# A two-layer sequence model on one core: a product moved to GpSimd, sums, row maxima and a projection in other places, and the end in another order

## The reference, cut to what matters

```python
xn = layernorm(x)
# layer 0: a selective scan with 16 states over 256 channels, beside a top-1 mixture of 8 experts
hs, gate = split(xn @ in_proj_w.T, 2)                       # 256 wide each
u  = silu(conv1d_depthwise(hs, conv_w, taps 4) + conv_b)
x_dbl = u @ x_proj_w.T                                      # 64 + 16 + 16
dt = softplus(rmsnorm(x_dbl[:64]) * dt_ln_w @ dt_proj_w.T + dt_proj_b)
Bm, Cm = rmsnorm(x_dbl[64:80]) * b_ln_w, rmsnorm(x_dbl[80:]) * c_ln_w
h_t[n] = exp(-dt * exp(A_log[n])) * h_{t-1}[n] + dt * u * Bm[n]       # along the sequence
y = sum_n h[n] * Cm[n] + u * D
x = x + (y * silu(gate)) @ out_proj_w.T + expert_e(xn)      # e = argmax of the gate's logits
xn = layernorm(x)
# layer 1: attention in a window of 32 to both sides, 16 heads of 8, beside a SwiGLU block of 384
q, k, v = xn @ Wq + bq, xn @ Wk + bk, xn @ Wv + bv
p = softmax(q k^T / sqrt(8) + mask(|i - j| <= 32))
x = x + (p v) @ Wo + bo + (silu(xn @ wg.T) * (xn @ wu.T)) @ wd.T
```

## Time and profile before

| | |
|---|---|
| median of three runs | 1000.43 us (1000.12, 1000.43, 1002.18) |
| the profiled execution's own time | 1001.08 us |
| its span in the profile | 999.3 us |
| TensorE busy (matmuls) | 797.0 us, 80% of the span |
| TensorE weight loads | 548.1 us, 55% |
| VectorE busy | 758.9 us, 76% |
| ScalarE busy | 638.5 us, 64% |
| GpSimd busy | 437.8 us, 44% |
| mean granted clock of TensorE | 0.928 of full speed |
| chain that ended last, by engine | PE 36%, DVE 20%, POOL 15%, issue 13%, ACT 9%, DMA 3% |

### The profile page before, as it was taken

The page is one execution under the profiler, slowest core; times in us unless marked ns, Lnnn a source line. Parts: engine busy times, 40 slices in busy tenths (PEclk is TensorE's granted clock), DMA queues, the critical chain, the costliest instruction groups (busy, mean ns, idle before and its releaser), DMA issues.

```text
span 999.3 us, 15614 instructions
## 1 busy us (share of the span) xinstructions
PE 797.0 (80%) x5226; PEld 548.1 (55%) x5226; DVE 758.9 (76%) x1059; ACT 638.5 (64%) x1976; POOL 437.8 (44%) x248
## 2 busy tenths in 40 slices
PE   0955689677489798979898989898988996798775
PEld 0732678676165366546555655565556554555543
DVE  7569445543577988899888888998898788887485
ACT  0224356644269767966796689578947893795563
POOL 2257432110556337624851584258425852672100
...
GB/s 209 189 119 189 206 265 310 244 213 153 65 123 97 85 100 134 104 80 121 130 93 97 127 124 70 106 129 131 52 124 142 104 47 121 157 112 23 18 11 12
DMA packets 85952, 123.20 MB, mean 123 GB/s; under 512 B 8560, under 2 KB 43760, under 8 KB 85744
## 3 DMA queue, kind: packets, MB, share of 16 engines
...
...
## 4 chain that ended last, share of the span: by engine, by line
PE 36%; DVE 20%; POOL 15%; issue 13%; ACT 9%; DMA 3%; SPq 3%; DVEq 0%; POOLq 0%; ACTq 0%
POOL hc L1221 8%; DVE hst L823 7%; PE y_bank L1319 4%; PE more L1451 4%; PE work L1338 4%; DVE dBu L815 3%; POOL xs_d L1189 3%; ACT pexp L1123 3%; POOL x_res L1205 2%; SPq L604 2%; ACT dA L1045 2%; PE work L1364 1%; PE work L1297 1%; PE work_l L1290 1%; PE work L1463 1%
## 5 line engine op out<-in xcount | busy, mean ns | idle before, releaser
L1221 POOL TENSOR_TENSOR hc<-hst,bcr 128x1024 f32<-128x1024 f32 x116 | 276.9, 2387 | 397.6 <-DVE dBu L815 375.3
L823 DVE TENSOR_TENSOR_SCAN hst<-dA,dBu 128x1024 f32<-128x1024 f32 x128 | 291.7, 2279 | 0.9 <-ACT dA L1045 0.3
L1045 ACT ACTIVATE dA<-dt,neg_a 128x511 f32<-128x511 f32 x256 | 170.7, 724 | 13.3 <-DVE hst L823 10.7
L815 DVE TENSOR_TENSOR dBu<-dtu,bcr 128x1024 f32<-128x1024 f32 x128 | 161.8, 1264 | 19.6 <-DMA bcr<-bc_d 9.7
L1319 PE MATMUL y_bank<-pk,hc 128*128 128x128 f32 x1024 | 144.2, 287 | 27.1 <-POOL hc L1221 26.3
L1319 PEld LDWEIGHTS y_bank<-pk,hc 128*128 128x128 f32 x1024 | 122.2, 148 | 64.8 <-POOL hc L1221 39.4
L1451 PE MATMUL more<-pk,pexp 128*96 128x128 f32 x480 | 103.5, 290 | 26.2 <-ACT pexp L1123 20.7
L1451 PEld LDWEIGHTS more<-pk,pexp 128*96 128x96 f32 x480 | 56.5, 125 | 66.1 <-issue 29.2
L1136 ACT COPY pT<-more 96x512 f32<-96x512 f32 x120 | 69.9, 583 | 34.5 <-PE more L1451 34.2
L1123 ACT ACTIVATE pexp<-work_l,nmax 128x96 f32<-128x96 f32 x240 | 78.5, 345 | 9.5 <-DVE nmax L970 9.4
L1123 ACT ACTIVATE pexp<-work,nmax 128x96 f32<-128x96 f32 x240 | 77.7, 335 | 2.6 <-DVE nmax L970 2.6
...
## 6 DMA issues: line engine op xcount, KB each, us to landing
bcr<-bc_d SPq DMA_DIRECT2D x128, 512.0 KB, 5.1
...
```

Source lines behind the costliest of these rows:

```text
L815: v.tensor_tensor(dBu[:], dtu[par], bcr[n % RING][:, 0:1, :].to_broadcast([P, NH, L]), ALU.mult).then_inc(s_dBu, 1)
L823: v.tensor_tensor_scan(hst[n % 2][:].rearrange("p h t -> p (h t)"), dA[n % 2][:].rearrange("p h t -> p (h t)"), dBu[:].rearrange("p h t -> ...
L1045: s.activation(dA[n % 2][:, h, 1:L], dt[par][:, h, 1:L], ACT.Exp, scale=neg_a[:, h, n:n + 1]).then_inc(s_dA, 1)
L1221: g_.tensor_tensor(hc[n % 2][:], hst[n % 2][:], bcr[n % RING][:, 1:2, :].to_broadcast([P, NH, L]), ALU.mult).then_inc(s_hc, 1)
```

## The change

It does the following.

1. The product with C of state 15 goes from VectorE's `step` to GpSimd's `times_c`, which then waits for scan 15.
2. `up2` of sequences 0 to 5 goes from bank 0 to bank 5, the pre lane's bank. `xnT` of the pre lane now waits until `up2` has been read.
3. In slots 7, 8 and 10 the sum stands behind the transposes `turn`. The row maximum of slot 8 stands directly behind the scan.
4. `xdr` goes from the end of slot 9 to directly behind scan 8 in slot 10, and `bc` to the end of slot 10. That holds for turn -1 too.
5. The SwiGLU chunks of sequence 6 leave turn 7 and go to the head of `LAST`, with banks of their own (`FFN_BANK`). `rdT` of that sequence stands behind them.
6. In `LAST` the SwiGLU chunks of sequence 7 go to t = 2 to 7, with buffers of their own (`fth_of`, `fsg_of`, `fh_of`), `avg` to 7, the four `fin` blocks to 8 to 11 one by one, `ffn_down` in four units to 12 to 15. The finish is written out, with the values of groups 13, 14 and 15 in three banks.

```diff
-MID = {2: [("scan", "slots", 0)], 8: [("pre", "ss", 0)], 18: [("pre", "dw", 0)], 20: [("pre", "dt", 0)], 23: [("pre", "dtu", 0)]}
+MID = {2: [("scan", "slots", 0)], 8: [("pre", "ss", 0)], 10: [("pre", "xdr", 0)], 18: [("pre", "dw", 0)], 20: [("pre", "dt", 0)], 23: [("pre", "dtu", 0)]}
...
-        9: [("pre", "xdr", 0), ("pre", "bc", 0), ("scan", "rows", 1)],
-        10: [("pre", "zg0", 0)], 11: [("pre", "sg0", 0), ("scan", "rows", 2)],
+        9: [("scan", "rows", 1)],
+        10: [("pre", "bc", 0), ("pre", "zg0", 0)], 11: [("pre", "sg0", 0), ("scan", "rows", 2)],
...
-ROWMAX_MID = (20,)
+ROWMAX_MID = (8, 20)
+SUM_LAST = (7, 8, 10)
...
+LAST_AT = {0: [("v2", 0), ("v3", 0)],
+           2: [("fg", 0), ("fu", 0)], 3: [("fs", 0), ("fh", 0)], 4: [("fg", 1), ("fu", 1)], 5: [("fs", 1), ("fh", 1)],
+           6: [("fg", 2), ("fu", 2)], 7: [("fs", 2), ("fh", 2), ("avg", 0)],
+           8: [("fin", 0)], 9: [("fin", 1)], 10: [("fin", 2)], 11: [("fin", 3), ("y_out", 0)],
+           12: [("ffn_down", 0)], 13: [("ffn_down", 1), ("proj", 0)], 14: [("ffn_down", 2), ("proj", 1)], 15: [("ffn_down", 3)]}
...
-        units += [("scan", "sum", m) for m in range(N - 1) if SUM_AT[m] == slot]
+        sums = [("scan", "sum", m) for m in range(N - 1) if SUM_AT[m] == slot]
+        units += sums if slot not in SUM_LAST else []
...
         units += [(lane, "turn", g) for lane, g in of("exp", slot)]
+        units += sums if slot in SUM_LAST else []
...
-    out = [("y_end", 0, a), ("rdT", 0, f), ("gated", 0, a), ("yT", 0, a)]
-    out += [(name, 0, a) for name in ("out", "x1", "ln_a", "ln_b", "q", "k", "v0", "v1")]
+    out = [("y_end", 0, a), ("fg", 0, f), ("fu", 0, f), ("gated", 0, a), ("fs", 0, f), ("fh", 0, f), ("yT", 0, a),
+           ("fg", 1, f), ("out", 0, a), ("fu", 1, f), ("x1", 0, a), ("ln_a", 0, a), ("fs", 1, f), ("fh", 1, f),
+           ("fg", 2, f), ("fu", 2, f), ("ln_b", 0, a), ("fs", 2, f), ("fh", 2, f), ("rden", 0, f), ("rdT", 0, f)]
+    out += [(name, 0, a) for name in ("q", "k", "v0", "v1")]
...
+    out += [(name, k, a) for name, k in (
+        ("exp", G - 1), ("scale", G - 2), ("turn", G - 2), ("values", G - 3), ("proj", 2), ("own", G - 4),
+        ("scale", G - 1), ("turn", G - 1), ("own", G - 3), ("values", G - 2), ("y_last", 2), ("own", G - 2),
+        ("values", G - 1), ("own", G - 1), ("proj", 3), ("y_last", 3))]
...
-           "oL": 0, "gate0": 1, "up0": 2, "gate1": 0, "up1": 1, "gate2": 2, "up2": 0}
+           "oL": 0, "gate0": 1, "up0": 2, "gate1": 0, "up1": 1, "gate2": 2, "up2": 5}
...
+FFN_BANK = {"gate0": 5, "up0": 6, "gate1": 7, "up1": 5, "gate2": 6, "up2": 7}
...
             if key == "xnT":
-                done1(eng, b + LAG["pre"] - 1 - LAG["finish"], "fin")
+                done1(eng, b + LAG["pre"] - 1 - LAG["attn"], f"up{HC - 1}")
...
+                    if it == B - 1 and lane == "attn" and name in FFN_UNITS:
+                        continue
...
-                if n == N - 1:
-                    dve.wait_ge(s_h, b * N + N)
-                    dve.wait_ge(s_hc, b * N + N - 1)
-                    dve.wait_ge(s_ys, b * (N + 1) + N - 1)
-                    v.tensor_tensor(hc[n % 2][:], hst[n % 2][:], bcr[n % RING][:, 1:2, :].to_broadcast([P, NH, L]),
-                                    ALU.mult).then_inc(s_hc, 1)
...
-                pool.wait_ge(s_dBu, b * N + n + 2)
+                if n < N - 1:
+                    pool.wait_ge(s_dBu, b * N + n + 2)
+                else:
+                    pool.wait_ge(s_h, b * N + N)
...
-                    if name == "product" and k < N - 1 and not ((b == 0 and k < DVE_C)):
+                    if name == "product" and not ((b == 0 and k < DVE_C)):
                         times_c(b, k)
```

More of the change, by code:

```diff
@@ L215, in keys @@
     return {"scores": [f"s{k}"], "turn": [f"pT{k}"], "fg": [f"gate{k}"], "fu": [f"up{k}"], "ln_b": ["xnT"], "fin": ["fin"] if k == NT - 1 else [], "yT": ["yT0", "yT1"],
-            "values": ["oL" if k == G - 1 else "oK"], "proj": [f"fin{k}"] if k >= 2 else []}.get(name, [])
+            "values": [{G - 3: "oK", G - 2: "oM", G - 1: "oL"}.get(k)], "proj": [f"fin{k}"] if k >= 2 else []}.get(name, [])
 L1_BANK = {"yT0": 1, "yT1": 2, "out": 0, "xnT": 1, "q": 0, "k": 1, "v0": 2, "v1": 0, "v2": 1, "v3": 2, "rdT": 2, "fin": 5,
            **{f"s{k}": k % 2 for k in range(G)}, **{f"pT{k}": 2 for k in range(G)},
-           "oL": 0, "gate0": 1, "up0": 2, "gate1": 0, "up1": 1, "gate2": 2, "up2": 0}
+           "oL": 0, "gate0": 1, "up0": 2, "gate1": 0, "up1": 1, "gate2": 2, "up2": 5}
 LAST_BANK = {"yT0": 1, "yT1": 2, "out": 0, "xnT": 1, "q": 3, "k": 4, "v0": 2, "v1": 6, "v2": 7, "v3": 5,
              **{f"s{k}": (0, 1, 3, 4)[k % 4] for k in range(G)}, **{f"pT{k}": (2, 6)[k % 2] for k in range(G)},
-             "oK": 0, "oL": 1, **{f"gate{k}": 5 for k in range(HC)}, **{f"up{k}": 7 for k in range(HC)}, "fin2": 5, "fin3": 7}
+             "oK": 0, "oM": 3, "oL": 1, **{f"gate{k}": 5 for k in range(HC)}, **{f"up{k}": 7 for k in range(HC)}, "fin2": 5, "fin3": 7}
+FFN_BANK = {"gate0": 5, "up0": 6, "gate1": 7, "up1": 5, "gate2": 6, "up2": 7}
 L1_ORDER = [(turn - LAG[lane], key) for turn in range(1, B) for lane, name, k in PLAN
-            if lane in ("attn", "late", "finish") and 0 <= turn - LAG[lane] for key in keys(name, k)]
+            if lane in ("attn", "late", "finish") and 0 <= turn - LAG[lane]
+            and not (turn == B - 1 and lane == "attn" and name in FFN_UNITS) for key in keys(name, k)]
 L1_ORDER += [(b, key) for name, k, b in LAST for key in keys(name, k)]
@@ L234, in l1_bank @@
         return LAST_BANK[key]
+    if b == B - 2 and key in FFN_BANK:
+        return FFN_BANK[key]
     return L1_BANK[key]
@@ L390, in program @@
         o_last = hst[0][:, 0, :]
+        fh_last = [dA[0][:, 0, :], dA[0][:, 1, :], dA[1][:, 0, :]]
         k_flat_b = rbuf[:, 1, :]
@@ L980, in layer1 @@
                         done1(dve, b, f"up{k - 1}")
-                    v.scalar_tensor_tensor(fsg[:], fth[:], 1.0, w1k(b, f"gate{k}")[:], ALU.add,
+                    v.scalar_tensor_tensor(fsg_of(b), fth_of(b), 1.0, w1k(b, f"gate{k}")[:], ALU.add,
                                            ALU.mult).then_inc(free1(b, f"gate{k}"), 1)
@@ L1461, in layer1 @@
                     key, j = (f"gate{k}", 0) if name == "fg" else (f"up{k}", 1)
+                    if b == B - 2 and key == "gate0":
+                        pe.wait_ge(s_h, B * N)
+                        pe.wait_ge(s_free0, B * L0_N)
                     take1(pe, b, key)
```

46 lines of the change are left out of this document (23 added, 23 removed).

## The result

The changed kernel takes 991.62 us (median of four runs, 990.82 to 993.64), the kernel before 1001.3 us in runs on the same chip. The ratio is 0.9895 (95% interval 0.9874 to 0.9916): some 10 us faster, a little under half of the 20.4 us forecast, and outside the range of 974 to 989 us. The profiled execution took 993.64 us with a span of 991.8, the slowest of the four; its span is 7.5 us shorter than that of before, so about 2 us of what follows are that execution's own.

The account below looks back on a forecast made before the run. It saw VectorE hardly idle in turns 1 to 7, with waits at the turn, slots 8 to 12, lead-in and end. Terms -13.2 + 0 - 1.5 + 3.0 + 0.5 - 9.2 = -20.4 us gave 980.1 us, range 974 to 989.

Parts of the forecast that it names:

- The turn: Between sequences: product 15 on GpSimd and up 2 in the pre bank save VectorE's product and two waits, 13.2 us together.
- The lead-in: Before the first scan: `xdr` falls behind six routing operations, so scan and scatter chains start 3.0 us later.
- (f): Finish after the last copy: values 14 and head 13 no longer wait, 11.6 us for 15.0, saving 3.3 us.
- VectorE and GpSimd exclude one another: A VectorE instruction with two SBUF inputs and a GpSimd one reading SBUF exclude one another for the whole instruction.
- Sums behind the turns, row maximum 8, `xdr` to slot 10: Slots 8 to 12: the wait before `xdr` becomes a longer one before row maximum 6, 0 us per turn.
- B: Rival, chance 0.20: low clock falls on TensorE's work behind the turn, about 12 us given back, 992 us.
- (d): End: TensorE no longer idles before q and k, 2.0 us at full clock for 3.78; 1.4 of 1.7 counted.
- (e): The end's groups: spread chunks add 3.9 us, single `fin` and `ffn_down` blocks 3.6, old waits go: -2.5 us together.
- Turn 7: Row maximum 3 precedes the `dBu` waiting for its row's DMA, so exponential 3 starts earlier: -1.5 us.

Follow-up runs that it names:

- the gate projection ahead: The changed kernel with the first gate projection moved directly behind `xdr`, ahead of the sum of scan 7: 983.03 us, ratio 0.9805.
- the first and third of the remedies together: Changed kernel, row maximum 8 behind the increments, `pick` behind `xdr`, chunks whole: 976.15 us; the same plus gate projection ahead of sum 7: 974.01 us.
- The three parts alone: The kernel before with only product 15 and bank edits: 986.2 us; only the slot tables: 1004.88 us; only the new end: 996.98 us.

## Why the prediction was wrong

**Right:** the sign, and the largest term. *The turn* was forecast at 13.2 us for all; the profiles show 13.0 in the six turns behind sequence 1 to 6, and the two edits by themselves give 15.3 us (1001.46 to 986.2), within the noise of such medians. The split holds in the turn itself (1.3 us for the product, 0.8 for the bank), but not in the whole kernel: I added the bank's gain to the product's, and by the medians the product has all of it, since what the bank wins comes back at x1. *The lead-in*, 3.0 us, measured 2.8 over eighteen profiles, and its route as well. *The finish* (f), 3.3 us forecast, 3.5 in the profile; over all profiles, with the old finish at 13.6 to 15.0 us and the new at 11.4 to 11.8, it is 2.6. *VectorE and GpSimd exclude one another*: product 15 was drawn out as forecast.

**The step that failed first:** "*Sums behind the turns, row maximum 8, `xdr` to slot 10* ... Value taken: 0 per turn (bounds -0.44 ... and +0.3)". I had every start right: the sum of scan 7 came 0.2 us later behind scan 7 than before, the transposes of 0.44 us stood ahead of it. Where the clock held, in turn 4, scan 7 to scan 9 took 13.61 us against 13.86 before, within my bounds. What I did not count is what TensorE does with its head start. Row maximum 3 is early, so exponential, scores and transposes are, and TensorE reaches the sum of scan 7 with 2.10 us to wait instead of 1.10. Its clock falls, and the sum and the gate projection behind, which scan 9 hangs on, take 1.5 us longer in five turns of six. The six turns lost 4.8 us from scan 7 to scan 10. By medians the early row maximum costs the changed kernel 8.9 us (991.6 against 982.7) and the kernel before 3.2 us. I had priced low clock as a rival at the turn alone (B, 12 us given back), from a row on which it could be seen there, and let this stretch, where the trace of before shows full clock, have bounds that left it out. That the time, 991.62 us, is so near to B's 992 is luck: of B's mechanism this execution shows 2.5 us in turn 7, 0.7 in turn 3 and the half clock of (d).

**Second:** (d), "I count 1.4 of the 1.7" for q and k at full clock. They took 3.78 us again in the changed kernel and 2.0 in five of the eleven other profiles with the same instructions there (the row maximum back, the gate projection ahead, the whole chunks, and the first and third of the remedies together); what decides it I could not tell. The bound of that term allowed for it, the value did not.

**Third:** (e), -2.5 us, measured +0.7. The waits at `fin` and `ffn_down` fell as forecast. The chunks were mis-sized: split over two rounds a chunk delays TensorE by VectorE's `fs` and `fh` and then VectorE by TensorE's gate and up, 2.4 to 3.0 us and once 4.7 with half clock (by how much longer its rounds are than the 2.23 us of a plain one), where the whole chunk cost 2.2; of this I had counted one wait of 1.3. The other part of the term came as forecast: a block of `fin` or `ffn_down` makes its group 0.4 us longer (2.63 against 2.23), 0.45 forecast. With the chunks whole the groups come to 2 us less than before, near my value.

**Turn 7**, -1.5 us: the wait went as forecast (scan 7 to scan 10 is 2.2 us shorter), and the half clock behind the turn took 2.5 us at x1, as in rival B, but of that size in this turn alone.

The three parts alone add up to -15.3 + 2.8 - 5.1 = -17.6 us; together they gave 9.7. Of the missing 8 us some 6 go with the row maximum, which costs 3 us by the medians in the kernel before and 9 in the changed one. The difference does not lie at slots 8 to 12: there it costs 7.7 us in the one and 7.5 in the other, and the clock falls about as often, in 11 turns of 12 and in 14 of 18. It lies elsewhere, most of it at q and k: in the kernel before their half-clock stretches grow fewer with the early row maximum, in the changed one they were more, by 4.2 us each way in the profiles. That is read from one profile of each, and what decides q and k from one execution to the next stays open; so does the rest of the 8 us, which is not clear of the spread of such medians.
